# A perceiver layer with 16 heads and 8 experts on one core: expert weights split in five blocks instead of six, and a reordering of queues around them

## What is computed

```python
# x (32, 64, 512), ctx (32, 1601, 512), float32
x = x + xattn(layernorm(x), ctx)         # one-head attention over 1601 rows, four features, @ W_qv
x = x + attn(layernorm(x))               # 16 heads of 32, causal over 64 tokens
x = x + ffn(layernorm(x))

# ffn: 8 experts, top 2 of them for each token, and a shared expert
probs = softmax(x @ w_router.T); weight, idx = top_k(probs, 2); weight /= weight.sum(-1)
y_e = square(relu(x_e @ w1_stack[e].T)) @ w2_stack[e].T      # (tokens, 512) by 512x512, twice
moe = sum over the two experts of weight * y
shared = square(relu(x @ ws1.T)) @ ws2.T                     # 1024 wide
return shared + moe
```

## Times and profile before

| | us |
|---|---|
| median of three runs | 1411.37 |
| the three runs | 1411.92, 1405.96, 1411.37 |
| the profiled execution | 1410.75 |
| span of its instructions | 1409.0 |

### The profile page before, as it was taken

How to read it: one execution, slowest core, us unless ns; L and a number is a source line. 1 busy time by engine, 2 the same in 40 slices (tenths; PEclk the granted TensorE clock), 3 DMA queues, 4 the chain that set the end, 5 groups by cost and what they waited for, 6 DMA issues and landing times.

```text
span 1409.0 us, 21536 instructions
## 1 busy us (share of the span) xinstructions
PE 1334.6 (95%) x7482; PEld 843.0 (60%) x7483; DVE 727.9 (52%) x1357; ACT 345.5 (25%) x608; POOL 178.4 (13%) x201
## 2 busy tenths in 40 slices
PE   6889999999999999999999999999988999999995
PEld 2334444444444444467888888899875666666772
DVE  3235455444444444468788786675433444444335
ACT  2101111111111111325444444323122222222210
POOL 0000000000000000013111116204310000000065
PEclk9999999999999999999999999999999999999998
DMA  9999999999999999509656541415297999999786
GB/s 366 392 395 396 388 392 395 393 392 386 385 388 375 359 366 367 217 3 378 226 218 220 217 171 61 170 71 187 112 342 241 345 332 318 300 304 309 258 283 186
DMA packets 122050, 408.72 MB, mean 290 GB/s; under 512 B 12400, under 2 KB 32880, under 8 KB 122000
## 3 DMA queue, kind: packets, MB, share of 16 engines
q1 hardware_dynamic: 116880, 391.30, 75.9%
q0 software_dynamic: 5120, 16.78, 3.5%
HBM read 345.65 MB, written 62.39 MB: 290 GB/s over the span
## 4 chain that ended last, share of the span: by engine, by line
PE 62%; DMA 13%; SPq 8%; DVE 7%; issue 5%; ACT 3%; POOL 2%; POOLq 0%; DVEq 0%; ACTq 0%
PE ps L1766 11%; PE ps L1830 10%; PE ps L1706 10%; DMA arena<-moe_in 10%; PE ps L1820 6%; PE ps L1719 4%; PE ps L1727 4%; PE ps L1716 3%; PE ps L1667 3%; SPq L507 2%; SPq L369 2%; DMA arena<-ctx_t 2%; PE ps L2111 2%; ACT arena L677 2%; DVE zero L1496 2%
## 5 line engine op out<-in xcount | busy, mean ns | idle before, releaser
L1766 PE MATMUL ps<-arena 128*64 128x512 f32 (+1 forms) x832 | 195.0, 601 | 4.1 <-DMA arena<-ctx_n 4.0
L677 ACT ACTIVATE arena<-ps 128x512 f32<-128x512 f32 x112 | 64.8, 597 | 520.2 <-PE ps L1667 195.4
L1706 PE MATMUL ps<-arena 128*64 128x512 f32 (+1 forms) x1024 | 180.5, 509 | 7.2 <-DMA arena<-ctx_t 4.3
L1830 PE MATMUL ps<-split 128*128 128x256 f32 x1344 | 170.0, 285 | 3.7 <-DVE split L1180 3.6
L1820 PE MATMUL ps<-split 128*128 128x512 f32 x672 | 164.9, 399 | 5.7 <-DVE split L1428 3.7
L1830 PEld LDWEIGHTS ps<-split 128*128 128x128 f32 x1344 | 163.5, 191 | 9.8 <-issue 8.9
L1820 PEld LDWEIGHTS ps<-split 128*128 128x128 f32 x672 | 124.5, 190 | 35.6 <-DVE arena L1434 4.1
L1706 PEld LDWEIGHTS ps<-arena 128*64 128x64 f32 x1024 | 66.2, 138 | 130.2 <-issue 122.4
L1106 DVE SCALAR_TENSOR_TENSOR arena<-arena,hbar 128x512 f32<-128x512 f32 x128 | 90.5, 748 | 94.9 <-PE ps L1727 90.6
L1766 PEld LDWEIGHTS ps<-arena 128*64 128x64 f32 (+1 forms) x832 | 58.7, 138 | 119.5 <-issue 111.5
L1039 DVE TENSOR_REDUCE small<-ps 128x1 f32<-128x1601 f32 x16 | 29.2, 1824 | 139.0 <-PE ps L1706 139.0
(11 more groups left out here) (184 smaller groups left out, 1727.9 us busy)
## 6 DMA issues: line engine op xcount, KB each, us to landing
arena<-ctx_t SPq DMA_DIRECT2D x128, 800.5 KB, 19.2
arena<-ctx_n SPq DMA_DIRECT2D x128, 768.0 KB, 15.9
split<-wx_low SPq DMA_DIRECT2D x78, 768.0 KB, 6.3
wx_high<-split SPq DMA_DIRECT2D x16, 768.0 KB, 4.6
wx_low<-split SPq DMA_DIRECT2D x16, 768.0 KB, 3.7
moe_in<-zero SPq DMA_DIRECT2D x3, 3328.0 KB, 20.5
arena<-moe_in SPq DMA_DIRECT2D x156, 64.0 KB, 4.3
moe_out<-arena SPq DMA_DIRECT2D x39, 256.0 KB, 5.8
```

The lines of the kernel that those rows point to most:

```text
L677: return nc.scalar.activation(o, i, ACT.Copy)
L1706: last = mm(bank(n)[S * h:S * (h + 1), 0:w], qT[:, k, S * h:S * (h + 1)], ctxT[h][:, k, at_j:at_j + w], start=(k == 0), stop=(k == KD - 1))
L1766: last = mm(bank(7)[S * h:S * (h + 1), :], ET[0:w, c, S * h:S * (h + 1)], ctxN[h][0:w, c, :], start=(c == 0), stop=(c == JC - 1))
L1830: last = mm(dst[:, 2 * P * m:2 * P * (m + 1)], w[a][:, k, c], tokens[b][:, k, :], start=(k + i == 0), stop=(k == KD - 1 and i == 2))
```

## The change

1. **Five blocks.** KA = 3 blocks of an expert's first matrix and KB = 2 of its second are split; the second matrix keeps two whole blocks. There are 12 sets instead of 16: eight of three blocks, and four that hold two blocks of each of two experts. `part_products` takes the number of split blocks. The low parts of a second product are 512 KB. `interT` grows to two blocks and gets a place of its own.
2. **Places of the sets in self-attention.** Two sets a round, in rounds 1 to 6 on DVE: one between the two query sums, one after the low part of the first attention tile. On ACT one before `attn_high` and one after the keys, the first in round 0 already.
3. **SP's loop over the groups.** The tokens of g+2 are issued first, then the low parts of g's second product; the store of `moe_out` comes before the low parts of g+2's first product. The shared weights are fetched in every second pass from g = 6 on, not in the passes 2 to 13.
4. **DVE before the experts.** `tokens_T(0)` comes after the last `shared_rest`, not before it.
5. **Gathers.** The slot numbers are read in place; the copies, their semaphore and the loop are gone.

```diff
-KS = KD - 1
-SETS = ((), (0, 1), (2, 3, 4), (5, 6, 7), (8, 9, 10), (11, 12, 13), (14, 15), ())
+KA, KB = 3, 2
+NS = E + E // 2
...
+            def set_of(n):
+
+                w, e = (0, slice(n, n + 1)) if n < E else (1, slice(2 * (n - E), 2 * (n - E) + 2))
+                return w, e, (KA, KB)[w]
...
             for g in range(GT):
                 e = expert_of(g)
-                sp.wait_ge(in_done, g + 1)
-                load_low(1, e, g % 3)
                 if g + 2 < GT:
                     sp.wait_ge(xgT_ready, g + 2)
                     load_slots(g + 2)
+                sp.wait_ge(in_done, g + 1)
+                load_low(1, e, g % 3)
                 if g > 0:
                     if g + 2 < GT:
                         e = expert_of(g + 2)
+                    sp.wait_ge(y_ready, g)
+                    sp.dma_start(moe_out[P * (g - 1):P * g, :], yg).then_inc(y_out, 16)
+                    if g + 2 < GT:
                         sp.wait_ge(y_done, g)
                         load_low(0, e, (g + 2) % 3)
-                    sp.wait_ge(y_ready, g)
-                    sp.dma_start(moe_out[P * (g - 1):P * g, :], yg).then_inc(y_out, 16)
-                if 2 <= g < 2 + KD + KF:
-                    sp.dma_start(*ws_parts[g - 2]).then_inc(ws_in, 16)
+                if g >= 6 and g % 2 == 0 and g < 6 + 2 * len(ws_parts):
+                    sp.dma_start(*ws_parts[g // 2 - 3]).then_inc(ws_in, 16)
...
-                for k in range(2):
-                    nc.gpsimd.tensor_copy(idx[k][i][:, :], slot_i[k][:, bass.ds(4 * n + i, 1)]).then_inc(gidx_ready, 1)
-                pool.wait_ge(gidx_ready, 8 * n + 2 * i + 2)
-                pool.sem_inc(pool_go, 1)
                 for k in range(2):
                     nc.gpsimd.indirect_dma_start(
-                        y01[k][i], None, moe_out, bass.IndirectOffsetOnAxis(ap=idx[k][i][:, :], axis=0)
-                    ).then_inc(y01_in[i], 16)
...
+                        y01[k][t % 4], None, moe_out, bass.IndirectOffsetOnAxis(ap=slot_i[k][:, t:t + 1], axis=0)
+                    ).then_inc(y01_in[t % 4], 16)
...
             def stage_b(n, now, last, first=False, second=False, more=True):
...
-                    round_part(parts, 0)
+                    if more:
+                        round_set(2 * n - 1)
                     attn_high(a - 2, 0, second)
                     pt_copy(a - 1, False)
-                    round_part(parts, 1)
...
-                round_part(parts, 2)
...
+                if 2 * n < NS:
+                    round_set(2 * n)
...
             dve.wait_ge(slots_zeroed, 48)
+            shared_rest(TA // 2 - 1)
             tokens_T(0)
-            shared_rest(TA // 2 - 1)
             tokens_low(0)
...
-                mm(dst, raw, raw_w, start=True, stop=False)
+                for k in range(n, KD):
+                    mm(dst, raw(k), raw_w(k), start=(k == n), stop=False)
                 waits[0]()
-                for k in range(KS):
+                for k in range(n):
                     mm(dst, parts[0][:, k, :], high_w(k), start=False, stop=False)
```

146 lines of the change are left out of this document (74 added, 72 removed).

## The result

| | before | forecast | after |
|---|---|---|---|
| median, us | 1411.4 (20 executions) | 1375 (1367 to 1388) | 1404.1 (1393.1 to 1407.9, 20 executions) |
| profiled execution, its span | 1410.75, 1409.0 | | 1405.91, 1404.0 |
| start of the experts | 1058.8 | 1051.8 | 1056.8 |
| length of the experts' stretch | 278.9 | 261.7 | 273.0 |
| from there to the end of the span | 71.3 | 59.3 | 74.3 |

After against before is 0.9939, with an interval of 0.992 to 0.9957. The time lies outside the forecast range. The three lengths come from TensorE's timeline: the first product of group 0, the end of the last expert product, and the end of the span. The medians stand beside the ratio as they were recorded; the ratio is not exactly the quotient of the two medians.

The account below looks back on a forecast made before the run. Bounds: the token-DMA loop in the experts, GpSimd's gathers at the end, and shorter TensorE waits earlier. Self-attention -3.5, shared expert -3.5, experts -17 and end -12 sum to -36 us: 1375 us, range 1367 to 1388.

Parts of the forecast that it names:

- the four waits: Self-attention: TensorE's 0.9 us idle times ending the four rounds with three sets each would go, -3.6 us.
- the +1.3: Self-attention round 0: ACT rounds a set, 1.47 us, ahead of tokens TensorE needs for round 1; cost taken as +1.3.
- the 1.44 given back: Self-attention round 1: TensorE's 1.44 us wait shrinks as the first subtraction no longer stands in it; taken as -1.2.
- the shorter pause: End of the shared expert: TensorE's 3.71 us pause shrinks by 2.2; avoiding the slow clock behind it taken as -1.3.
- the token loop would stop being the bound: Experts: issue to transposition falls from 6.99 to 4.7 us, under the 5.7 that TensorE's need leaves the tokens.
- 6.47 us as TensorE's need: Experts: TensorE's work per group, 6.30 us plus 0.17 for one float32 block replacing three passes.
- (a): Rival, experts: the token loop stays the bound, -6 in place of -17, 1386 us; chance 0.12.
- (d): Rival, experts: the float32 block could cost more than 0.86 us where two follow each other; counted inside 4 us.
- the thinnest cover here: Experts: a first product's low parts, queued behind the store, have 7.4 us to land against a 6.3 median; costed at nothing.
- Rival (c): Experts: low parts landing after 7.4 us stop TensorE in every first product's third pass, up to 1451 us; chance 0.04.
- Rival (b): End: gathers don't get closer, each issue taking 1.35 us, -6.7 in place of -12, 1380 us; chance 0.13.
- TensorE's bound: End: last product starts no sooner than 1383.7, takes 7.1 us, then sum and store to 1394.7; gain at most 14.3.

Follow-up runs that it names:

- a_same: The changed kernel run again unedited, on another chip: 1394.5 us, 0.9864 of the kernel before.
- c_same: The changed kernel run again unedited, on yet another chip: 1406.6 us, 0.9959 of the kernel before.
- a_hook: Changed kernel with TensorE's load of the second product's expert number ahead of the first product's last low-parts wait: 1388.6 us, 0.9826 of the kernel before.
- a_wslate: Changed kernel with the twelve shared-weight loads issued in passes 27 to 38, not every second pass from 6 to 28: 1409.1 us, 0.9982 of the kernel before.
- a_regs: Changed kernel with TensorE's register load of the second product's expert number ahead of the whole first product: 1406.6 us, 0.9982 of the kernel before.

## Why the prediction failed

1. **Self-attention and the shared expert, -7.0 forecast, +0.1 measured from the first load of raw weights.** The start of the experts is 2.0 us sooner in the first profile, but that is the earlier head of that execution, which is luck; in a_same and c_same the experts start within 0.2 us of before. Each part of the sum came: the four waits, the +1.3, the 1.44 given back, the shorter pause without its loss of clock (1.4 us off the waits, where 2.2 were forecast). The step that failed is one left out: "ahead of the tokens that TensorE needs for round 1" was followed along ACT and DVE, but the set's own load not along SP's queue. The change asks for the third set in round 1, not in round 2, and its load stands behind the zero writes. That cost a wait of 3.75 us and the half clock behind it. With the zero writes moved the term was -6.2 to -6.3 in five profiles.
2. **The experts, -17 forecast, -5.9 in the first profile.** That the token loop would stop being the bound was right, and 6.47 us as TensorE's need was right too: the float32 block costs what was forecast, so rivals (a) and (d) fall. "I cost this at nothing, and it is the thinnest cover here" is the step that failed. The 6.3 us of the earlier trace rows lump the loads of both products; the first product's alone had 5.6 in the median before, and in their new place behind the store they took 6.9, not less. In 10 of 36 passes they took more than the 7.4 that were thought free, 8.5 at most. Rival (c) had the place right, but not the size. In only six passes do they land so late that the third part starts with them, and such a delay doesn't add up over the passes. What costs most is the step behind, by the register load at that wait, which no part of the forecast had: 6 of the missing 11 us (a_hook, 5.6). Late low parts alone don't account for it: in the first profile two thirds of that step's excess fall in passes whose read took longer than 0.4 us. The other 5 us are in part the low parts' own waits; the shared weights make them later (a_wslate), and what else does was not separated.
3. **The end, -12 forecast, +3.0 in the first profile, -8.5 to -9.9 without the stall.** GpSimd's part was right: the last gather is issued 19 us sooner. Rival (b) falls by its size: L674 has 1031 ns each, and two pairs stand 2.6 us apart in the median. But what it says of single issues is true in these rows: the 17 issues that overlap a mix took 1.09 us in the mean and up to 1.47, the 15 others 0.96. The Trainium skill ("SBUF — State Buffer", SBUF: two separate sides) says that GpSimd and VectorE share a port pair that one holds for a whole instruction. The longer issues agree with it. But ten of the 17 stayed under 1.1 us, and the mixes take 752 ns with and without copies, so these rows bear it out only in part. The step that failed is TensorE's bound, "its last product can't start before 1390.77 - 7.10 = 1383.7, takes 7.1 at full clock": it let the products ahead of the last one run as before. They crawled for 18 us, at the half clock for most of it, and the last one started at 1393.8. Without the stall TensorE is the bound, as forecast, but with 1.4 us for a tile whose load stands behind those of `x_away` and 1.6 us for DVE's square: 62, not 59.3. The stall, 12 us with its half clock, was foreseen nowhere, and I don't see a row of before that would have told of it.

Three smaller slips in the working changed nothing. A turn of the token loop of 7.7 us is that of the one group shown; 278.8 over 39 groups is 7.15. The cover of a second product's low parts adds the whole 1.38 of its float32r passes, but they are needed after 0.92 of it, so 6.6 us were free, not 7.0; they took 4.7 in the median and 6.4 at most. And two bad ends don't give 1382: those of the experts and the end alone make 1389.

Between the span forecast, 1372.8, and the one measured, 1404.0, are 31.2 us: 5.0 up to the start of the experts, 11.3 in them and 15.0 at the end. By size that is the stall (about 12), the register load (6), the zero writes (6), the low parts and what else delays a pass (5), the waits of the last tiles (3) and the shared expert's waits (1), less 2 for the earlier head of that execution.

## What to carry over

When a load is asked for sooner, follow its own queue back to what stands ahead, not only the engines that wait for it. Cover for a wait has to include all that the engine's own queue does between that wait and the next matmul. A register load behind a wait that comes late, or one that itself takes long, was paid in 17 of 38 passes here. It cost 5.6 us less behind matmuls already queued and ahead of the wait (a_hook); in front of the whole product (a_regs) the cost came back. Compare a stage by its own length from a mark that no edit touches, not by the time at which it ends. An engine off the path that is made faster can slow the one on it: take the profile on more than one chip before crediting the gain, and try a small pause.

## What the hardware showed

TensorE can be slowed to one weight load and matmul per 0.7, 1.4 or 2.1 us, with no semaphore waited for, while GpSimd issues indirect gathers at 2.6 to 2.8 us a pair. It began 32 to 36 us after the first gather in all five cases, lasted 13 to 19 us and could end before the gathers did (a_regs: at 1377.0, last gather 1383.5). Two small copies per pair (3.1 us a pair) kept it away on a chip that stalled. My first idea was that its instructions came late. The queue that the profile calls q8 instruction moves packets of 16 KB, 28 in the whole run; that they are TensorE's isn't shown. One arrived in front of the stall (first fence, DMA queues of the changed kernel from 1344 to 1352) and none was moved in it (second fence, from 1366 to 1384), and TensorE was back at full pace 1.3 us before the next one at 1385.2. So a late packet of that queue didn't end the stall. The DMA engines weren't fuller than in a_same, 275 against 292 GB/s. What the 0.7 us are is open.

```profile
q8 instruction: 1, 0.02, 0.8%
```

```profile
q0 software_dynamic: 1076, 3.54, 68.3%
q1 hardware_dynamic: 804, 1.45, 21.2%
```

A read of a number from SBUF into a register took TensorE 0.30 us in the median, and up to 1.15 us in the changed kernel; the cause of the long ones is open.
